# Written-out group loops and operands read in place in a gated cross-attention kernel on one core

## What is computed

```python
x = x + tanh(g_xattn[0]) * _L0_xattn_ref(_layernorm(x), ctx_1024, fside, fside, mask, mask, Wq, Wk, Wv, Wo, ...)
x = x + tanh(g_ffn[0]) * _L0_ffn_ref(_layernorm(x), W_qkv, b_qkv, W_gate, b_gate, W_experts, b_experts)

# _L0_xattn_ref, for each of 4 layers i:
q = einsum('bfd,dnh->bfnh', _norm(x), Wq[i]) * 64 ** (-0.5)
k = einsum('btd,dnh->btnh', src, Wk[i]);  v = einsum('btd,dnh->btnh', src, Wv[i])
hbias = relu(dist[..., None] @ Wth[i] + bth[i])            # 32 features per score
qs_bias = (hbias @ Wto[i] + bto[i])[..., 0]
w = softmax(einsum('btnh,bfnh->bnft', k, q) + bias + qs_bias[:, None])
x = x + einsum('bfnh,nhd->bfd', einsum('bnft,btnh->bfnh', w, v), Wo[i])
x = x + relu(_norm(x) @ Wf1[i] + bf1[i]) @ Wf2[i] + bf2[i]
```

## Time and profile before

| | us |
|---|---|
| median of 3 runs | 1383.88 (1382.38 to 1387.49) |
| the profiled execution, its own time | 1388.81 |
| its span, first to last instruction | 1387.1 |

### The profile page before, as it was taken

The page is one execution under the profiler, slowest core; times in us unless marked ns, Lnnn a source line. Parts: engine busy times, 40 slices in busy tenths (PEclk is TensorE's granted clock), DMA queues, the critical chain, the costliest instruction groups (busy, mean ns, idle before and its releaser), DMA issues.

```text
span 1387.1 us, 39817 instructions
## 1 busy us (share of the span) xinstructions
PE 1228.3 (89%) x11184; PEld 1013.8 (73%) x11184; DVE 1222.8 (88%) x4922; ACT 1064.8 (77%) x3353; POOL 834.8 (60%) x889
## 2 busy tenths in 40 slices
PE   1599989898989899898989898989898999788897
PEld 1377878787878787777878787878787878666665
DVE  4899989898989999898989898989898988579996
ACT  4588878787878888787878686878787876568886
POOL 3677767676767677676767676767676754211110
PEclk9899999999999999999999999999999999989999
DMA  5201000002110000021100101111101000000000
GB/s 153 67 7 30 16 27 12 29 12 76 44 31 12 23 19 22 20 68 34 31 25 13 29 12 31 57 47 28 31 12 42 12 12 9 5 22 19 18 20 9
DMA packets 69117, 41.06 MB, mean 30 GB/s; under 512 B 14841, under 2 KB 63873, under 8 KB 68993
## 3 DMA queue, kind: packets, MB, share of 16 engines
q1 hardware_dynamic: 68992, 39.84, 10.1%
HBM read 23.29 MB, written 1.05 MB: 18 GB/s over the span
## 4 chain that ended last, share of the span: by engine, by line
issue 27%; DVE 24%; ACT 18%; PE 17%; POOL 3%; DVEq 1%; DMA 1%; ACTq 0%; SPq 0%; POOLq 0%
ACT prob L802 10%; DVE bias_acc L951 4%; PE M L582 3%; ACT relu_z L785 3%; PE O L552 3%; DVE score L998 3%; DVE qT L1123 3%; DVE hid L1073 3%; DVE st L1016 2%; PE M L628 2%; PE M L560 2%; PE L L689 1%; ACT probT L809 1%; ACT oT L814 1%; DVE rs L1025 1%
## 5 line engine op out<-in xcount | busy, mean ns | idle before, releaser
L802 ACT ACTIVATE prob<-score,nmax 128x128 f32<-128x128 f32 x1024 | 396.7, 390 | 182.7 <-DVE nmax L998 177.3
L1396 POOL TENSOR_TENSOR prob<-prob,rinv 128x512 f32<-128x512 f32 x256 | 293.9, 1148 | 234.0 <-DVE rinv L1006 231.9
L951 DVE SCALAR_TENSOR_TENSOR bias_acc<-relu_z,cst,bias_acc 128x512 f32<-128x512 f32 x370 | 339.7, 918 | 9.7 <-ACT relu_z L785 0.2
L785 ACT ACTIVATE relu_z<-dist_g,cst 128x512 f32<-128x512 f32 x386 | 294.9, 804 | 16.9 <-DMA cst<-cst_all 16.9
L998 DVE CUSTOM_DVE_ANT_0 score<-L,bias 128x128 f32<-128x128 f32 x1024 | 233.8, 282 | 4.2 <-PE L L528 1.5
L802 ACT ACTIVATION_READ_ACCUMULATOR prob<-score,nmax 128x1 f32 x1024 | 193.2, 189 | 0.0
L1391 POOL TENSOR_TENSOR sd<-mv,half 128x1 f32<-128x1 f32 x128 | 105.6, 825 | 120.4 <-DVE mv L1018 117.6
L538 PE MATMUL T<-ident,prob 128*128 128x128 f32 x1024 | 163.9, 284 | 4.7 <-POOL prob L1396 3.8
L552 PEld LDWEIGHTS O<-probT,v 128*64 128x64 f32 x2048 | 109.3, 136 | 62.0 <-issue 54.4
L582 PE MATMUL M<-wv,ctxT 128*128 128x512 f32 x256 | 147.0, 658 | 7.7 <-DVE hid L1073 5.1
L528 PE MATMUL L<-kT,qT 64*128 64x128 f32 x2048 | 149.6, 286 | 0.0
(11 more groups left out here) (134 smaller groups left out, 2226.7 us busy)
## 6 DMA issues: line engine op xcount, KB each, us to landing
dist_g<-in_fside_BxSxS SPq DMA_DIRECT2D x16, 256.0 KB, 2.7
mask_g<-in_mask_Bx1x1xS_ff SPq DMA_DIRECT2D x16, 256.0 KB, 3.5
ctxT<-ctxT_all SPq DMA_DIRECT2D x64, 64.0 KB, 1.9
xs<-x_all SPq DMA_DIRECT2D x64, 64.0 KB, 1.8
x_all<-xs SPq DMA_DIRECT2D x64, 64.0 KB, 1.9
wk<-in_L_xattn_Wk SPq DMA_DIRECT2D x4, 512.0 KB, 3.7
wv<-in_L_xattn_Wv SPq DMA_DIRECT2D x4, 512.0 KB, 4.3
wq<-in_L_xattn_Wq SPq DMA_DIRECT2D x4, 512.0 KB, 5.0
```

Of the source, the lines that this page charges most:

```text
L785: nc.scalar.activation(relu_z[:, z_slot(g, k), :], dist_g[:, :, :], ACT.Relu, bias=cst[:, C_BTH + k:C_BTH + k + 1], scale=cst[:, C_WTH + k ...
L802: last = nc.scalar.activation(prob[:, c, m, :], score[:, c, m, :], ACT.Exp, bias=nmax[:, c, m:m + 1], scale=-1.0, accum_out=rsum[:, c, m:m ...
L951: vec.scalar_tensor_tensor(out=bias_acc[:, :], in0=relu_z[:, z_slot(g, k), :], scalar=weight, in1=bias_acc[:, :], op0=ALU.mult, op1=ALU.ad ...
L1396: gp.tensor_tensor(prob[:, c, :, :], prob[:, c, :, :], rinv[:, c, :].rearrange("p (m o) -> p m o", o=1).broadcast_to([P, 4, P]), ALU.mult) ...
```

## The change

`walk` calls the steps of every group with a number instead of looping with a register; SP's program is written out likewise. With the group known, x, the context and the constants are read and written in the big tiles; the tiles `xs`, `ctxT`, `cst` and `x4`, their copies and their semaphores go. The places of the waits on the copies are taken by waits on who wrote the data: `moments` waits for `ln_done` and for `resid2` of the same batch one layer back, `f_first` for `resid2`, ACT's first `relu` of a group for `cst_in` and `dist_in`, POOL's first `product` for `cst_ready`. At the start SP no longer waits for the constants between its loads. The loads of weights, dist, mask and `xr` stay, in the same order.

```diff
@@ walk
             for i in range(first, GROUP):
                 step(0, i)
-            with eng.Fori(1, groups - 1) as g:
+            for g in range(1, groups - 1):
                 for i in range(GROUP):
                     step(g, i)
@@ new helpers
+        def x_of(g, i):
+            return x_all[:, (GROUP * g + i) % BATCHES, :]
+        def ctxT_of(g, i):
+            return ctxT_all[:, (GROUP * g + i) % BATCHES, :]
+        def cst(g, col):
+            return cst_all[:, g // GROUPS_PER_LAYER, col:col + 1]
@@ SP, start
-            load_dist_rows(0)
+            load_dist(0)
             sp.dma_start(x_raw[:, :, :], x.rearrange("b s d -> s b d")).then_inc(x_in, 16)
-            wait_first(sp, consts, cst_in, 64)
-            load_cst(0, C_WTH, C_WTO, dist_in)
-            load_wto(0)
+            load_mask(0)
             sp.dma_start(c_raw[:, :, :], ctx_in.rearrange("b t d -> t b d")).then_inc(c_in, 16)
-            wait_first(sp, consts, cst_ready, 4)
-            load_cst(0, C_PW, C_ALL, cp_in)
             load_k(0)
             load_vq(0)
             load_q(0)
-            sp.wait_ge(cT_kept, 4)
-            load_ctx_slot(0, 0)
-            load_ctx_slot(0, 1)
-            wait_first(sp, consts, ln_done, GROUP)
-            load_x_slot(0, 0)
-            load_x_slot(0, 1)
@@ SP, group(l, gg)
-                    if there(g, i - 2):
-                        store_x_slot(g, i - 2)
-                    if there(g, i + 2):
-                        if first and i + 2 == GROUP:
-                            wait_first(sp, consts, ln_done, BATCHES)
-                        load_x_slot(g, i + 2)
-                        load_ctx_slot(g, i + 2)
...
                     load_dist(g + 2)
-                    load_cst(g + 2, C_PW, C_ALL, cp_in)
                     wait_first(sp, consts, bias_done, g + 2)
-                    load_wto(g + 2)
+                    load_mask(g + 2)
@@ SP, load_rows and the layers
-                wait_first(sp, consts, xs_out[s], (g + i // GROUP + UNITS // GROUP - F_GROUPS + 1) * 16,
-                           fx1, after(g, i - GROUP, 1))
-                sp.dma_start(x4[:, s, :], x_all[:, bass.ds(b, 1), :].rearrange("p o d -> p (o d)")).then_inc(x4_in[s], 16)
+                wait_first(sp, consts, fx1, after(g, i - GROUP, 1))
...
-                    with sp.Fori(1, GROUPS_PER_LAYER - 1) as gg:
+                    for gg in range(1, GROUPS_PER_LAYER - 1):
                         group(l, gg)
                 group(l, GROUPS_PER_LAYER - 1, last=l == LAYERS - 1)
-            for i in range(GROUP, GROUP + 2):
-                store_x_slot(GROUPS - 1, i - 2)
@@ TensorE, keys
-                    pe.wait_ge(ctx_slot[i % 2], (g * 2 + i // 2 + 1) * 16)
...
-                project(M0, wk, ctxT[:, i % 2, :], a).then_inc(k_done, 1)
+                project(M0, wk, ctxT_of(g, i), a).then_inc(k_done, 1)
@@ ACT, relu
-                    act.wait_ge(dist_in, (g + 1) * 32)
+                    act.wait_ge(cst_in, 64)
+                    act.wait_ge(dist_in, (g + 1) * 16)
@@ DVE, term
-                    dve.wait_ge(cv_in, (g + 1) * 32)
                     wait(dve, bias_done, g)
@@ DVE, moments
-                    dve.wait_ge(xs_in[i % GROUP], (g + i // GROUP) * 16 + 16)
+                    if GROUP * g + i < BATCHES:
+                        dve.wait_ge(ln_done, GROUP * g + i + 1)
+                    wait(dve, resid2, after(g, i - BATCHES, 1))
...
-                vec.bn_stats(st[:, a, s, :], xs[:, i % GROUP, :]).then_inc(bn[a], 1)
+                vec.bn_stats(st[:, a, s, :], x_of(g, i)).then_inc(bn[a], 1)
@@ DVE, residual sums
-                    vec.tensor_tensor(xs[:, (i - 2) % GROUP, :], M2[:, 0:P], xb[:, i % 2, :], ALU.add).then_inc(resid2, 1)
+                    vec.tensor_tensor(x_of(g, i - 2), M2[:, 0:P], xb[:, i % 2, :], ALU.add).then_inc(resid2, 1)
@@ DVE, f_first
-                    dve.wait_ge(x4_in[i % GROUP], (g + i // GROUP) * 16 + 16)
+                    dve.wait_ge(resid2, UNITS - BATCHES + after(g, i, 1))
@@ POOL, product
-                wait_first(pool, consts, *((dist_in, (g + 1) * 32, cp_in, (g + 1) * 16) if k == first_k(g) else ()),
+                wait_first(pool, consts, *((dist_in, (g + 1) * 16, cst_ready, 4) if k == first_k(g) else ()),
                            pool_clamp, pool_count(g, k - 1))
```

More of the change, by code:

```diff
@@ L239, in block_program @@
         w_k, w_v, w_q, w_o, w_f1, w_f2, w_b1, w_b2 = [sem("w_" + n) for n in "k v q o f1 f2 b1 b2".split()]
-        cst_in, cst_mul, cst_ready, dist_in, cv_in, cp_in = [sem(n) for n in ("cst_in", "cst_mul", "cst_ready", "dist_in", "cv_in", "cp_in")]
+        cst_in, cst_ready, dist_in, cv_in = [sem(n) for n in ("cst_in", "cst_ready", "dist_in", "cv_in")]
         z_done, term_done, bias_done = sem("z_done"), sem("term_done"), sem("bias_done")
         pool_mul, pool_clamp, pool_sum = sem("pool_mul"), sem("pool_clamp"), sem("pool_sum")
-        xs_in = [sem(f"xs_in{i}") for i in range(GROUP)]
-        xs_out = [sem(f"xs_out{i}") for i in range(GROUP)]
-        ctx_slot = [sem(f"ctx_slot{i}") for i in range(2)]
         bn, var, sdev, sdeps, rstd, h_done = [[sem(f"{n}{a}") for a in "ab"] for n in ("bn", "var", "sdev", "sdeps", "rstd", "h_done")]
@@ L258, in block_program @@
         f_consts, f_in, f_gate_in, tanh_done = sem("f_consts"), sem("f_in"), sem("f_gate_in"), sem("tanh_done")
-        x4_in = [sem(f"x4_in{i}") for i in range(GROUP)]
         xr_in = [sem(f"xr_in{i}") for i in range(GROUP)]
@@ L581, in values @@
                     pe.wait_ge(k_kept[1], after(g, i, 1))
-                mm((M0 if a else M1)[:, :], ctxT[:, i % 2, :], wv[:, a * 512:(a + 1) * 512], start=True, stop=True).then_inc(v_done, 1)
+                mm((M0 if a else M1)[:, :], ctxT_of(g, i), wv[:, a * 512:(a + 1) * 512], start=True, stop=True).then_inc(v_done, 1)
             def queries(g, i, a):
@@ L782, in relu @@
                 if k == 0:
-                    act.wait_ge(dist_in, (g + 1) * 32)
+                    act.wait_ge(cst_in, 64)
+                    act.wait_ge(dist_in, (g + 1) * 16)
                 wait(act, term_done, vec_count(g, k + 1 - Z_SLOTS))
-                nc.scalar.activation(relu_z[:, z_slot(g, k), :], dist_g[:, :, :], ACT.Relu, bias=cst[:, C_BTH + k:C_BTH + k + 1],
-                                     scale=cst[:, C_WTH + k:C_WTH + k + 1]).then_inc(z_done, 1)
+                nc.scalar.activation(relu_z[:, z_slot(g, k), :], dist_g[:, :, :], ACT.Relu, bias=cst(g, C_BTH + k),
+                                     scale=cst(g, C_WTH + k)).then_inc(z_done, 1)
             def relus(g, i, q):
@@ L1111, in step @@
                     dve.wait_ge(wo_done, after(g, i - 1, 1))
-                    vec.tensor_tensor(xs[:, (i - 1) % GROUP, :], M2[:, 0:P], xs[:, (i - 1) % GROUP, :], ALU.add).then_inc(resid1, 1)
+                    vec.tensor_tensor(x_of(g, i - 1), M2[:, 0:P], x_of(g, i - 1), ALU.add).then_inc(resid1, 1)
                 if cur:
@@ L1421, in add @@
                 if k == first_k(g):
[L1423 removed]
+                    pool.wait_ge(cv_in, (g + 1) * 16)
                     wait(pool, bias_done, g)
@@ L1466, in step @@
                         pool.wait_ge(w_b2, layer_of(g, i - 1) * 16 + 16)
-                    gp.tensor_tensor(xb[:, (i - 1) % 2, :], xs[:, (i - 1) % GROUP, :], bf2b[:, :], ALU.add).then_inc(xb_done, 1)
+                    gp.tensor_tensor(xb[:, (i - 1) % 2, :], x_of(g, i - 1), bf2b[:, :], ALU.add).then_inc(xb_done, 1)
                 if early:
```

50 lines of the change are left out of this document (11 added, 39 removed).

## The result

The changed kernel takes 1344.86 us (median of 4 runs, 1342.64 to 1346.65) beside 1385.68 us of the kernel before: a ratio of 0.971 with a 95% interval of 0.968 to 0.974. The saving is 40.8 us by medians. Between the two profiled executions, 1388.81 and 1342.64 us, it is 46.2 us, where the sum of the prediction was 55.9. The time lies at the slow edge of the range, and the forecast of 1328.0 us was 17 us too low.

The account below looks back on a forecast made before the run. TensorE and DVE were both taken as nearly full, with DVE idle at each group's back jump. Savings of 49.2 + 2.6 + 4.1 = 55.9 us off the 1383.88 us median gave 1328.0 us, range 1312 to 1345 us.

Parts of the forecast that it names:

- Groups written out: Four-layer part: 13 back jumps go, saving 49.2 us, 32.4 of it idle DVE and 16.8 TensorE's low clock.
- the rule on branches: Skill's 51 ns per unconditional branch, 108 ns per compare-and-branch: 13 rounds would give 2 us, not 49.2; the prediction rejected it.
- Constants in place of register arithmetic: Four-layer part: wait numbers written into instructions gain zero, at most 7 us, and nothing below zero.
- The use of 68.36 us as the length of a jump-free group: Middle groups: the group from 125.12 to 193.48 us, without a back jump, taken as each written-out group's length.
- Rival (c): More than forecast: register work on the path (7 us) and groups of 67.70 us (9.2 more), 1311.8 us; chance 0.10.
- Rival (a): Clock stays low in part, or the 16.8 us belong to the group's start; only idle goes, 1344.8 us; chance 0.07.
- Rival (b): Slower by code fetch: 58 more blocks at up to 2.5 us stall TensorE, up to 1473 us; chance 0.05.
- the bound of 58.4: Four-layer part: upper gain in us if every group runs like group 0, straight code in 67.70 us.
- Rival (d): Another late thing, such as the dist or mask load, replaces the jump's idle time; about 1377 us; chance 0.03.
- Copies in place: x, context and constants used in the big tiles without slot copies: zero gain, no engine waits for them mid-step.
- Start: Kernel start: relu no longer waits for the constants' copy; gain 2.6 us at ln_rs, between 1.9 and 3.7.
- Last part: MoE and small attention: one back jump fewer gains 2.3 us, the x4 copy wait 1.8 us, together 4.1 us.

Follow-up runs that it names:

- the control at another place: Changed kernel with the always-met DVE wait ahead of the mid-step term after the second norm's statistics instead: 0.9727 against the kernel before, 1346.22 us.
- the delay on POOL: Changed kernel with the always-met DVE wait, plus an always-met wait on POOL before the first norm's one-column power: 0.9719 against the kernel before, 1347.45 us.
- the extra wait: Changed kernel plus an always-met DVE wait on consts ahead of the first term in steps 1 to 3 of a group: 0.9579 against the kernel before, 1325.90 us.
- the first experiment: Kernel before with the loops of TensorE, DVE, ACT and POOL written out, SP's loop and all slot copies kept: 0.9745, 1347.81 us.
- the kernel with the copy: Changed kernel with DVE's h2T copy out of PSUM moved before the step's first term: 0.9648 against the kernel before, 1334.54 us.

## Why the prediction was right and wrong

*Groups written out: right mechanism, and one term mis-sized.* DVE's own jump is what made it idle (all but DVE written out: the 31.6 us stay; DVE alone: they go), and the clock did the rest (1.2 us per fall, forecast 1.3). The 3.78 us per jump came back in steps 3 and 0 (20.8 is the middle of its range): 20.8 to 18.23 and 18.13 to 16.86, together 3.8 us. The middle part went from 71.87 us per group ((1131.35 - 125.12) / 14) to 69.08: 39.1 us saved, forecast 49.2. The missing 10.1 us are 14 groups at 69.08 - 68.36 = 0.72 us. The jump instruction takes 0.07 us; the rule on branches that the prediction set against the change prices this alone, and what cost time is the idle stretch behind it.

*"Constants in place of register arithmetic ... zero" and "Below zero I see nothing, since instructions only go away": the step that failed.* It cost 0.46 us in each of steps 1 and 2, 0.92 us per group, of which step 0 and the part of step 3 ahead of `bias` gave back some 0.2. That DVE's term now begins 0.06 us ahead of the power in place of 0.04, and that the power takes 1.10 us for it, is shown, by the wait on DVE (back to 0.55 us, 19 us saved), by the control at another place (nothing), and by the delay on POOL (back to 1.07 us, all of it lost again). That written-out code on DVE is enough for it is shown by the kernel with DVE alone written out. The register instruction is in the trace: 40 ns ahead of this term in every kernel with DVE in a loop, with the term at 0.22 us behind `mv`; a wait of 21 ns in its place where DVE is written out, with the term at 0.20. No run puts that one instruction alone back, so it is the likely cause of the 0.02 us and not a tested one; the extra wait does the same job.

*The use of 68.36 us as the length of a jump-free group* failed with it. That group contains no jump, but DVE had entered its loop, so it ran in the loop's form. And the trace of before had shown the loss. Group 0 is straight code with constant numbers, and I had looked at its sum alone, 67.70 us, as the favourable end. POOL's timeline of the kernel before, first in group 0, then in the loop:

```profile
89.90 1.10 POOL L1391 TENSOR_TENSOR sd<-mv,half 128x1 f32<-128x1 f32 x1 [1.64 <-DVE mv L1018]
...
106.89 1.10 POOL L1391 TENSOR_TENSOR sd<-mv,half 128x1 f32<-128x1 f32 x1 [1.64 <-DVE mv L1018]
...
159.02 0.55 POOL L1391 TENSOR_TENSOR sd<-mv,half 128x1 f32<-128x1 f32 x1 [1.64 <-DVE mv L1018]
```

Its steps 1 and 2 took 16.83 and 16.99 us against 16.51 in the loop. A straight group with full steps would then have been 16.9 + 17.0 + 17.0 + 18.2 = 69.1 us, and the forecast 1338. The sum of group 0 was short only because its step 0 has less to do (16.5 us).

*Rival (c)* was half right: the good end of 67.70 us per group exists (67.7 with the extra wait, four-layer part 58.1 us shorter, against the bound of 58.4), but the change as made does not reach it. *Rival (a)* gives the measured time, 1344.8 us, for a reason that did not occur: the clock did not stay low. *Rival (b)*: q8 brings 92 blocks (forecast 83). The prediction looked at q8 alone. With DVE alone written out q8 has 25 blocks as in the kernel before, so DVE's written-out code adds nothing to q8, and the fetch that DVE seems to wait for in the loop is on q14, which the prediction passed over with "only q14 is there". In the changed kernel both queues bring code without a wait that shows: the steps with the extra wait are as short as the loop's, 16.50 us, with the same 92 blocks. A cost of fetching turned up where the prediction did not look for it, in a longer loop. *Rival (d)* fell with the first experiment.

*Copies in place: right*, zero in the middle part. The one group of 73.0 us in the kernel with copies says that the chain of slots could cost something now and then.

*Start: about right in size* (2.15 us by the first `bias`, 57.42 to 55.27; forecast 2.6; the second run of the changed kernel has 55.78), less so in its steps. The relu came at 12.40 us (12.8) and the statistics at 16.46 us (16.7). The context came at 20.32 us (19.3): SP's queue was held by the issue of the mask from 5.05 to 12.16 us, and the transfers ran at 298 GB/s, not 276. DVE waited 2.83 us for relus behind the context's copies, and `ln_rs` came at 27.05 us, not 25.7.

*Last part: right in size partly by luck* (from the last `bias` to the end 255.73 to 250.59 us, 5.1 us; forecast 4.1). The wait at L1150 is gone and most `outF` come 10.15 us apart, which with it makes some 3 us. The rest lies in the passage to the last part, in which TensorE's clock is at the lower level for a shorter time. Windows of 25 us ahead of the first `outF`, before and after:

```profile
1206.35:1231.35 25.00, 20.38 (x137) 15.92 (x138) 14.47 (x67) 13.01 (x44) 2.11 (x4) 0.66 0.05 14
```
```profile
1165.04:1190.04 25.00, 19.74 (x152) 13.87 (x154) 17.14 (x79) 15.67 (x53) 2.65 (x5) 0.86 0.00 1
```

No experiment took this apart, and it is not steady. The kernels with the extra wait have the same last part as the changed one and need 253.5 and 252.6 us for it, with a clock of 0.66 and 0.73 in such a window. The kernel with only the loops written out keeps the copy to `x4` and needs 249.3 us. So the 1.8 us of the wait at L1150 are not shown as a gain by themselves. Open too are a few steps of the changed kernel that are 0.2 to 0.3 us longer than their neighbours, 1.0 us in all; they lie at the same steps with the extra wait.

The kernel with the extra wait, 1325.8 us, beats both the kernel before and the changed one.

## What to carry to other kernels

Idle without a releaser once per round of a loop belonged to the back jump of the fullest engine, 3.8 us each with what the clock added, and writing the loop out recovers it; a larger body with half of the jumps did not. At such a place look for a block on every instruction queue, not on one. Before you call an edit that only removes instructions free, look in the trace for the same code in the form it will get, and compare it instruction by instruction, not by its sum: a short instruction on another engine that takes 0.55 us in one place and 0.9 to 1.1 us in another is a race for something shared, and here 0.02 us decided it. After such a change, compare the mean durations of all groups of instructions on the two pages first; a cost that moved to another engine shows there, and a wait that costs nothing can turn the order back.

## What the runs showed of the hardware that I had not expected

The one-column power on POOL takes 0.55 us if it begins up to 0.045 us behind the recorded start of a term on DVE (267 powers), and 0.9 to 1.10 us if it begins from 0.058 us on while the term runs (1150 powers; all fourteen traces, and no start lies between). Every one of the long ones ends 0.41 us behind the end of the term: at 503.28 us behind 502.87 us in the changed kernel, where it began 0.06 us behind the term's start, and at 503.82 us behind 503.41 us with POOL's wait, where it began 0.09 us behind. So the later it starts the shorter it is, and its end hangs on the term. Behind a copy out of PSUM it takes 0.55 us at 0.06 us as well (43 powers).

The Trainium skill, SBUF — State Buffer, section SBUF: two separate sides, says that DVE and GpSimd share one pair of ports as an exclusive lock, that a DVE operation with two SBUF inputs takes it, and that whichever starts first keeps it for the whole instruction. The order that decides, the copy from PSUM that does no harm and the power whose end follows the term's agree. In the other direction it depends on the instruction. Behind a power that got in first the term takes 0.74 to 0.78 us (but for two of 1.60 us in the kernel with the copy) and is not held up for 0.55 us, which is not what the page says. Behind a large POOL instruction it is held. In the changed kernel:

```profile
145.76 1.27 POOL L1373 TENSOR_TENSOR pool_acc<-pool_acc,clamped 128x512 f32<-128x512 f32 x1
146.08 1.50 DVE L894 SCALAR_TENSOR_TENSOR bias_acc<-relu_z,cst_all,bias_acc 128x512 f32<-128x512 f32 x1
```

The term takes 1.50 us in place of 0.75 and ends 0.55 us behind the end of `pool_acc`. So do 130 terms there, which take 0.93 to 1.64 us: they start while a 128x512 instruction of POOL has 0.39 us or more left, and all end 0.54 or 0.55 us behind it. In the kernel before 129 terms do (0.53 to 0.55 us). Above 0.75 us each, that is 62 us of DVE's busy time before and 72 us after, and it is why the mean term grew. The kernel with the extra wait has these 72 us too and is the fastest, so the growth by itself is not what cost time; whether a better order of terms and POOL's work would save some of it was not tested. The lock itself is inferred; the runs show the durations and what decides them.

A back jump of DVE costs it some 2.5 us where a block of q14 follows it (2.8 to 3.1 us from the jump to the next instruction of its sequencer, with a body of one group and with one of two), and next to nothing where none does (0.32 us, at the jump of the last part in the kernel before). The loop of the last part is the same in every kernel with loops there, but with DVE's middle loop written out its jump costs DVE 2.8 us of idle time, and with two groups per round 3.3 us. So changing one loop can change what another one's jump costs. On TensorE a jump costs nothing that shows with one group, and 6 to 8 us with two. That the fetch makes up DVE's 2.5 us is read from these coincidences; no run changed it by itself.
